# A GNN and mixer network on one core: GpSimd waits for the preceding gather to land at every eighth gather of the second aggregation

## The reference, cut to what matters

```python
edge_index = jnp.stack([src, dst])             # 53125 edges, sorted by dst
xn = _layernorm(x, axis=-1)
support = xn @ weight                          # 256 x 256
msgs = support[src] * edge_weight[:, None]
agg = jax.ops.segment_sum(msgs, dst, num_segments=3125)
x = x + relu(agg) + mixer(xn)                  # the mixer ends in an MLP 256 -> 1024 -> 256
```

## Time and profile before

| | us |
|---|---|
| runs before: median of 3 | 2217.95 |
| runs before: lowest, highest | 2204.93, 2221.02 |
| span of the profiled execution, first to last instruction | 2177.7 |
| median less the profiled span: what lies around it, and spread | 40.2 |
| second aggregation in it, first to last step's matmul | 1301 to 1915 |
| GpSimd's gathers in it | 1301.1 to 1881.4 |

### The profile page before, as it was taken

One profiled execution on the slowest core, in us unless ns is written; L12 is line 12 of the kernel. 1 busy time (PEld: TensorE's weight loads), 2 busy tenths in 40 slices (PEclk: granted clock), 3 DMA queues, 4 the chain that ended last, 5 costly groups with the idle time before them and its releaser, 6 DMA issues. The chain is left out here.

```text
span 2177.7 us, 31463 instructions
## 1 busy us (share of the span) xinstructions
PE 1591.3 (73%) x7770; PEld 1251.9 (57%) x7770; DVE 1251.5 (57%) x3879; ACT 862.1 (40%) x2965; POOL 1067.5 (49%) x1173
## 2 busy tenths in 40 slices
PE   5635577766756786969999766877788887875892
PEld 4533444444444455959999654655566655664792
DVE  3523555555556687855777635454455455676435
ACT  2221656656555786635777431000011000143451
POOL 3751666666666500421222156666666666326351
PEclk8755668667777898989999867888888888896896
DMA  6741544444444302836555133333333333122786
GB/s 193 223 138 40 150 121 126 127 131 126 123 123 142 108 18 84 260 111 203 180 171 179 62 89 106 90 93 91 88 91 88 92 90 93 52 93 85 219 264 223
DMA packets 176882, 276.92 MB, mean 127 GB/s; under 512 B 28920, under 2 KB 132218, under 8 KB 176456
## 3 DMA queue, kind: packets, MB, share of 16 engines
q0 software_dynamic: 50352, 136.58, 21.8%
q1 hardware_dynamic: 82194, 94.23, 14.2%
q10 hardware_dynamic: 44166, 44.14, 6.1%
HBM read 202.35 MB, written 73.58 MB: 127 GB/s over the span
## 5 line engine op out<-in xcount | busy, mean ns | idle before, releaser
L501 POOL DMA_INDIRECT ring<-feat_d,src_lane x440 | 430.1, 977 | 281.8 <-issue 120.8
L1221 POOL DMA_INDIRECT rows<-xn_d,src_of x416 | 405.6, 975 | 228.7 <-issue 108.6
L1201 PE MATMUL bank<-ring,a_hot 128*128 128x260 f32 x880 | 318.9, 514 | 139.7 <-DVE ring L1100 81.4
L1392 PE MATMUL bank<-rows,big 128*128 x880 | 286.5, 443 | 129.1 <-DVE big L1300 68.9
L1130 ACT ACTIVATE ring<-ring 128x64 f32<-128x64 f32 x1540 | 375.3, 336 | 6.3 <-issue 5.6
L1201 PEld LDWEIGHTS bank<-ring,a_hot 128*128 128x128 f32 x880 | 207.5, 253 | 213.6 <-DVE ring L1100 95.7
L1309 DVE TENSOR_TENSOR big<-bank,big 128x256 f32 x440 | 186.7, 424 | 222.0 <-DMA m_bo<-in_L_mix_bo 114.7
L1392 PEld LDWEIGHTS bank<-rows,big 128*128 128x128 f32 x880 | 164.7, 209 | 225.9 <-issue 211.1
L1085 DVE TENSOR_TENSOR acc<-bank,acc 128x260 f32 x440 | 187.1, 425 | 143.2 <-DMA m_dst_bc<-dst_lo_d 60.9
L1362 ACT ACTIVATE big<-bank,a_col 128x256 f32<-128x256 f32 (+1 forms) x26 | 13.1, 552 | 416.9 <-PE bank L1407 177.5
L1300 DVE TENSOR_SCALAR big<-const,dst_lane,ew_lane 128x128 f32<-128x128 f32 x440 | 155.3, 353 | 1.0 <-PEq L95 1.0
(11 more groups left out here) (405 smaller groups left out, 2893.6 us busy)
## 6 DMA issues: line engine op xcount, KB each, us to landing
slots_d<-fold ACTq DMA_DIRECT2D x25, 1300.0 KB, 5.7
e_w_now<-in_L_ffn_w SPq DMA_DIRECT2D x56, 256.0 KB
a_dst_bc<-dst_lo_d SPq DMA_DIRECT2D x23, 512.0 KB
big<-in_L_ffn_W SPq DMA_DIRECT2D x16, 512.0 KB
e_x<-slots_d SPq DMA_DIRECT2D x56, 130.0 KB
ring<-feat_d,src_lane POOLq DMA_INDIRECT x440
rows<-xn_d,src_of POOLq DMA_INDIRECT x416
e_ys<-y_d SPq DMA_DIRECT2D x24, 256.0 KB
```

Of the source, the lines that this page charges most:

```text
L501: pool.indirect_dma_start(ring[:, q % RING, at, :], None, table, bass.IndirectOffsetOnAxis(ap=src_lane[:, n:n + 1], axis=0)).then_inc(gath ...
L1201: pe.matmul(bank[n % BANKS][:, 0:D + H], hot[:, q % HOTS, at, :], ring[:, q % RING, at, :], start=True, stop=True)\
L1221: pool.indirect_dma_start(rows[:, n % RING1, :], None, table, bass.IndirectOffsetOnAxis(ap=src_of[:, n:n + 1], axis=0)).then_inc(gathered[ ...
L1392: pe.matmul(bank[n % 4][:, 0:D], hot[:, n % HOTS, :], tile_of(rows, slots[n % 4]), start=True, stop=True)\
```

## The change

Ahead of every eighth gather (n = 24, 32, ..., 408) GpSimd waits until gather n - 1 has landed, that is until the semaphore of its slot has reached its full count. The wait stands behind the wait for room in the ring, which falls on the same n. No instruction is added to the other engines, none changes its place, and all data and sizes stay. The lines below L1291 move down by two, so that L1392 becomes L1394.

```diff
@@ -1289,6 +1289,8 @@
                     continue
                 if n % 4 == 0:
                     once(pool, summed, n + 4 - RING1 + T - 1)
+                if n % 8 == 0:
+                    pool.wait_ge(gathered[(n - 1) % RING1], (n - 1) // RING1 * 16 + 16)
                 fetch_rows(pool, rows, gathered, src_of, table, n)
```

## The result

| | before | after |
|---|---|---|
| median of the runs on one chip, us | 2214.84 (2204.93 to 2221.02, 4 runs) | 2240.44 (2236.46 to 2242.17, 4 runs) |
| ratio to before, 95% interval | | 1.0115 [1.0077, 1.0153] |
| span of the profiled execution | 2177.7 | 2240.4 |
| second aggregation, first to last step's matmul | 614.2 | 650.1 |
| gather 24 to gather 408, divided by 12 | 46.98 | 50.34 |

The changed kernel is 25.6 us slower at the median. I had forecast +7 us, 2225, in a range of 2204 to 2249; the time lies in the range, but on the slower side of 1%. In a later comparison the same two kernels were 5.9% apart; that is told with the second batch of experiments and is the larger lesson of this case. Ratios here leave out one run of all, 2180.93 us at a granted clock of 0.633 in the third batch, where the other runs of its kernel show 0.864 to 0.870.

A forecast was written before the change was run, and what follows sets the result against it. No engine is full: GpSimd's gathers and late TensorE matmul ends hold each other up in a loop. With waits, GpSimd's last gather delays TensorE's step 415 by +7.1 us; +7 on the median 2217.95 gives 2225, range 2204 to 2249.

The forecast's parts named there:

- Price of one wait: At each of 49 waits on GpSimd: 1.8 us of landing plus 0.30 to start the next gather, 2.1 us idle.
- Period: GpSimd's 32 steps in the second aggregation: pauses go from 7.04 to 8.4 us, the period from 46.85 to 48.25.
- Start: Gather 24 waits for gather 23, slowed by the MLP's weight loads, and begins at 1311.0 instead of 1307.38: +3.6 us.
- Who pays: TensorE catches up with GpSimd and waits for gather 415, so step 415 begins at 1902.1 instead of 1895.0.
- End: After 12 periods the last gather lands at 1902.0; TensorE's steps from 415 to the last take 20.3 us as before.
- The sum: Later begin of TensorE's step 415, 1902.1 - 1895.0 = +7.1 us, takes the profiled span from 2177.7 to 2184.8.
- rival (a): Slower: pauses of 2.1 us do not clear the hold-up; 2.3 us more per period, +28 us, 2246; chance 0.20.
- Profiled span and median: Median 2217.95 lies 40.2 us above the profiled span; called launch, ends and spread, untouched by the change.
- The hold-up: Ends of TensorE's matmuls come late while GpSimd issues without pause; 2.1 us pauses remove the 2 to 4 us gaps.
- (b): Faster: landing at its lower bound, idle 1.5 us per wait, period 45.8, -23 us, 2195; chance 0.15.
- (c): No change: TensorE's stretch has its own cause, period stays 46.85, 0 us, 2218; chance 0.10.
- +31 us: Sum if the skill page's 2.3 us landing estimate held, with 2.6 us idle per wait, in place of +7.

The follow-up runs named there:

- second batch of experiments: Comparisons on another chip, where the kernel before took 1893.84 us; the unaltered changed kernel took 2004.59 us, ratio 1.0593.
- third batch: Later runs on the first batch's chip, before at 1892.07 us; the 2180.93 us run had one landing wait in 32 gathers added to before, median 1916.68 us.
- swapped order: Changed kernel with the landing wait written ahead of the room wait: 2193.37 us, ratio to before 0.9987; on another chip 1984.00 us, ratio 1.0479.
- room wait alone: Kernel before plus a long-met wait for gather n - 8, making the room wait an instruction of its own: 1894.39 us, ratio 1.0002; repeated, 1892.61 us.

## Why the prediction was right and wrong

By its own steps:

- **Price of one wait: the step that failed.** The landing was right: 1.8 us after the issue's end (1936.69 to 1938.5; 1.75 to 1.9 at 44 of the 49 waits), as I had estimated from the traffic of the earlier trace rows. Wrong was "With 0.30 to get the next gather going". The 0.30 of the earlier trace rows is the distance between gathers that stand ready in the queue. The new wait is an instruction of its own, and behind it the distance is 0.7. The pause is 2.53 us, not 2.1. The swapped order bears this out: with pauses of 2.05 to 2.1 us its stage is 621.2, so 7.0 us over before, where I had worked out +7.1 for pauses of 2.1, and its start (+3.6) and period (48.19 to 48.25) fit too. That the two agree to 0.1 us is luck: by the medians the swapped order is 0.4 us over before, and the profiled execution of before was a fast one (below).
- **Period.** 50.34 us in place of 48.25, 2.09 more, twelve times 25.1: of this 48 x 0.43 = 20.6 are the mis-sized pause, and most of the other 4.5 are four gathers (143, 207, 255 and 367) that land 0.8 to 1.8 us later than the rest (the last section).
- **Start.** Gather 24 begins 10.9 us after the stage's first matmul, before 6.2: +4.7 where I had +3.6.
- **Who pays.** Right: TensorE stands behind the last gather, so that the stage is set by GpSimd. It begins step 415 3.0 us after that gather's end, where I had 1.9.
- **End.** "The steps from 415 to the last take the same 20.3 us as now" was short by 1.6: they take 22.0. The granted clock is 0.50 of full speed (1.2 GHz) in the last ten us ahead of step 415, in which TensorE stood waiting for rows again and again, last for 1.07 us, and for 4 us more, in which it was busy throughout; from 1956.4 on it is 0.99. In the swapped order it is at 1.00 from step 415 on (1907.78), and the same steps take 20.2 us. Windows of the change, then one of the swapped order:

```profile
1942.00:1952.40 10.40, 8.57 (x16) 3.98 (x16) 4.75 (x14) 0.81 (x2) 5.68 (x6) 0.50 0.35 88
1952.40:1956.40 4.00, 3.96 (x13) 3.52 (x14) 1.36 (x4) 0.09 (x1) 0.00 (x0) 0.50 0.03 6
1956.40:1962.40 6.00, 6.00 (x41) 5.58 (x40) 4.07 (x13) 2.40 (x8) 0.00 (x0) 0.99 0.00 0
```

```profile
1907.70:1911.70 4.00, 3.92 (x25) 3.45 (x26) 2.50 (x9) 0.62 (x2) 0.00 (x0) 1.00 0.02 6
```

- **The sum.** 7.1 + 1.1 + 25.1 + 1.1 + 1.6 = 36.0, the stage's +35.9 us. The medians differ by 25.6 only. The before that was profiled is one execution, and its stage need not be the median one's; the swapped order's stage is 7.0 over it as well, with medians 0.4 apart. That 10 us stays unexplained.
- **The range.** +25.6 is outside my own range of -5 to +15. It lies in 2204 to 2249 because that reaches past rival (a), whose mechanism did not occur: the kind of slowdown was foreseen, its size was covered for another reason. To slower by over 1% I had given 0.17, "(a) for the most part".
- **Profiled span and median.** I put the 40.2 us between them down to "launch, ends and spread". In the run after, time and span of one execution stand side by side: 2242.1 and 2240.4, so 1.7 us lie around a span. The 40.2 (37.1 with the fourth run) were spread almost alone: the execution that was profiled was faster than any that was timed.
- **The hold-up.** That pauses of 2.1 us clear it, rival (a) against, came out as forecast: the gaps of steps 26 to 29 are gone. The run without gathers and the one with shorter pauses bear out both halves of it at the upper level. But "the ends of matmuls are held up while GpSimd issues without a pause" is true at that level alone, and whether the landing or the quiet in the issue clears them is open.
- **The rivals.** (b) and (c) fell: the landing is not at its lower bound, and the period did not stay. The nearest was (a), 2246, in its size, by another mechanism: the hold-up was cleared, and the price of the cure was higher.
- **The Trainium skill's** page "DMA: Bandwidth & Descriptors" (Rules for kernel authors) says to issue early and wait late. At the lower level that is what the runs show, at 1.8 us and more per wait. The estimate of 2.3 us for the landing from its section "Anatomy of one DMA" is above the 1.8 measured from the end of the issue, and below the 2.8 from its start; that its +31 us lay nearer to the stage's +35.9 than mine did is a coincidence of two errors, in the landing and in the restart.

## What to carry to other kernels

A wait for a transfer that was issued just before costs its whole landing, here 1.8 us after the end of the issue; where it is wanted nevertheless, it should be the wait that the next instruction carries itself, and a wait that is met anyway the one that stands alone (written last, here), which is worth 0.4 to 0.5 us each time (20.6 / 49 by the medians, 2.53 less 2.05 by the pauses). Count such pauses against those that the engine makes already: here the same 49 waits cost +0 to +1% where GpSimd was being held up anyway and +5 to +6% where it was not. And before a change is aimed at a stall, see whether the stall is there on another chip or at another hour, and whether the trace is whole where it occurs: this one came and went, and the trace had gaps there.

## What the runs showed of the hardware

- Two levels of one kernel: 2214.84 and 2192.98 us in the first two comparisons, 1893.84 on another chip, and then 1892.07 on the chip that had given 2192.98. At the upper one the ends of TensorE's matmuls come microseconds late while GpSimd issues gathers, in both aggregations. A gap of 2.05 us in the issue after every eight gathers clears this, one of 0.8 us does not. In the same stretches the traces lack most of the semaphore updates (2691 of some 7990).
- GpSimd's queue runs some 12 us, eight gathers, ahead of the engine and works off waits there (1882.8 for the gather at 1894.86); in the kernel with the room wait alone it is 15 us. A wait that holds the queue costs 0.7 us of restart (at all 49) in place of 0.3.
- Gathers of one size do not all land alike. The one of chunk 255 lands 0.8 to 1.4 us later than most in every kernel that waits for it, at either level; with the change at the upper level, and with the swapped order at the upper and at the lower level, the pause behind it is:

```profile
1700.74 0.94 POOL L1221 DMA_INDIRECT rows<-xn_d,src_of  x1 [3.74 <-DMA rows<-xn_d,src_of]
```

```profile
1667.25 0.95 POOL L1221 DMA_INDIRECT rows<-xn_d,src_of  x1 [3.24 <-DMA rows<-xn_d,src_of]
```

```profile
1462.70 0.95 POOL L1221 DMA_INDIRECT rows<-xn_d,src_of  x1 [3.42 <-DMA rows<-xn_d,src_of]
```

The likely cause is a load of instructions. They come over DMA queues of their own; the page of the changed kernel has one with 71 packets of 16 KB:

```profile
q8 instruction: 71, 1.16, 0.2%
```

In the trace's packets, each of the four late gathers of the changed kernel (143, 207, 255, 367) has one packet of this queue on a DMA engine between its issue and its landing, begun 0.55 us before the issue's end to 1.0 us after it and 1.25 to 1.5 us long; the rows' own packets take 0.16 us at the median. In the swapped order too, at either level, every pause over 2.2 us has one. It is not the rows that are fetched: at gather 367 the swapped order has such a packet at the upper level, and a pause of 2.28 us, and none at the lower, and a pause of 1.98. This rests on where the packets fall in the traces; no run moved them.
